# Source rows of two edge networks: windows of 28 and 56 columns in place of seven of 28, one core of a Trainium2

## The chip, the core and the metric

The kernel runs on one core of a Trainium2 chip. Its time is the device time of one execution in microseconds (us). Three runs took 1854.54, 1861.17 and 1861.94 us; the median is 1861.17 us.

## What is computed

Four small graph networks run one after the other on 100,000 nodes of 32 features and 25,000 directed edges, sorted by destination. After each, the node rows are added or replaced and normalised:

```python
x = _layernorm(x + _L0_gnn_ref(x, edge_weight, edge_attr_3, edge_index, ...))
x = _layernorm(x + _L1_gnn_ref(x, edge_index))
x = _layernorm(x + _L2_gnn_ref(x, edge_index, edge_attr_32, ...))
x = _layernorm(x + _L3_gnn_ref(x, edge_attr3_2x32, src, dst, ...))
```

The change touches the third and the fourth, the two edge networks (layers 0 and 1 of `compact` and `WINDOW_ORDER` in the code). Both need the row of each edge's source node, `x[src]`, in its newest state. In the third an MLP of source row, destination row and edge attributes is followed by a maximum over the edges of a destination (`segment_max`). The fourth is an attention: scores, a softmax over the edges of a destination, messages, and a sum over them.

## The kernel before

**Layout.** Edge e lies in partition e // 196, column e % 196: 128 partitions by T = 196 columns, of 32 words each. `A_src` holds the source rows, `A_dst` the destination rows. A chunk is 28 columns (`GATHER_CHUNK`), seven of them; a quad is four columns, 49 of them.

**Source rows.** A node that is nobody's destination keeps a row that each core step can derive from the old one; only sources that are themselves destinations have to be read again, from a table in DRAM (`tables[3]`, `tables[4]`). By a count of the drawn inputs that is 22% of the edges. GpSimd (POOL) reads them with indirect DMAs (`gather`, L746), one for each column of 128 rows. So that it needs fewer than 196, the indices are packed: `make_windows` sorts them within each window of 28 columns to the window's first 16 places (`SLOTS_IN_WINDOW`), and DVE later moves the rows back to their own columns. Ahead of each gather stands a memset of a small tile that POOL itself waits for (`pause`, L736). If any window of any partition had more than 16 such sources, `n_short` would be set to T and the code would take its long branches.

**Moving.** `move_window(layer, c, k)` issues step k of window c: predicated copies (`copy_predicated`, L2253) that shift rows to the right by 16, 8, 4, 2 and 1 columns, of 12, 20, 24, 26 and 27 columns of 32 words, by masks from `make_windows`, and a last one (L2249) that puts the rows of all 28 columns in place. Step 0 first waits on DVE for the gathers of that window (`window_rows`). DVE's instructions run in the order of the code, so all that is written behind this wait waits with it.

**Order of work.** DVE, PE and ACT go through the network in turns, a quad each (`pipeline`); behind a turn, steps are hooked in by its number. In the third network turns 0 and 1 are the last two quads (columns 188 to 195) and turn q + 2 is quad q, up to turn 51 with the pipeline's lag. `bring_rows` (L2264) copies the quad's rows for PE, `take_maxima` (L2276, a scan over a chunk) follows behind turns 4, 11, 18, 25, 32, 39 and 46, the norm of each chunk after it (`center`, `variance`, `scale`). The windows are gathered in the order 6, 0, 1, ..., 5 (`WINDOW_ORDER`); windows 6 and 0 are moved in one go, window c = 1 to 5 in the six turns from 7c - 4 on. In the fourth network turn q is quad q (`bring_both`, L2368, and `score`); `HOOKS` gives the turns of the hooked steps: window c = 1 to 6 is moved behind turns 7c - 6 to 7c - 1, the softmax of chunk c behind turn 7c + 12, its messages are normalised behind 7c + 15 (L1495 with 56 words out), and the chunk's last step, `scale`, at 7c + 25 releases `final_ready`.

**End.** POOL scatters the finished rows of the fourth network to the output, one indirect DMA a column (L880), in the order of `LAST_ORDER`: columns 8 to 27, then chunks 1 to 6, then columns 0 to 7; ahead of each it waits for `final_ready`. These 196 scatters stand in POOL's queue behind the gathers of the fourth network.

## Time and profile before

| | |
|---|---|
| median of three runs | 1861.17 us |
| profiled execution, its span | 1863.2 us |
| POOL busy | 1400.9 us, 75% |
| DVE busy | 1344.3 us, 72% |
| PE busy | 729.3 us, 39% |
| ACT busy | 488.0 us, 26% |
| third network | 1084.6 us to 1359.2 us |
| fourth network | 1359.2 us to the end |

The times of the rows below come from one profiled execution; its span, from the first to the last instruction, is 1863.2 us and is its only time. POOL and DVE are both busy for about three quarters of it, and neither all the time: which of them sets the pace has to be read stretch by stretch. A third network's start is taken where DVE begins to spread the rows over the edges of a destination, and its end where it begins to do so for the fourth.

### The profile page before, as it was taken

Reading aid. Unit: us, or ns where it says so; the run is one execution under the profiler, and the core shown is the slowest. Engines: PE = TensorE matmul, PEld = TensorE weight load, DVE = VectorE, ACT = ScalarE, POOL = GpSimd, SP = SyncE. Lnnn points to the kernel's source line nnn. Section 1 sums busy time; section 2 is a strip of 40 time slices with the busy share of each in tenths; the row PEclk is TensorE's granted clock in tenths of the full one; section 3 lists DMA queues with packets and bytes.
Section 4 is the critical chain, followed back from the end, with each engine's and each line's share of the span. In section 5 each row is a group of like instructions: output and inputs, shape, how many; then the busy total and the mean of one; then the engine's idle time right before and its main releaser. Section 6 shows DMA issues by size and latency. Waiting matters only on the chain.

```text
span 1863.2 us, 14783 instructions
## 1 busy us (share of the span) xinstructions
PE 729.3 (39%) x3676; PEld 546.2 (29%) x3676; DVE 1344.3 (72%) x2600; ACT 488.0 (26%) x1014; POOL 1400.9 (75%) x2019
## 2 busy tenths in 40 slices
PE   7912555541450003605337001456605656551400
PEld 3301222220220003605326001355505655551400
DVE  9955999986999645775755882478785999986400
ACT  7822311110110013522334200233302343342100
POOL 8878887888888885868878558884068888888776
PEclk9966778775785556867678555677757776665655
DMA  8165511111111101412222330000001111110000
GB/s 321 38 211 194 184 32 32 32 26 17 26 20 50 42 20 59 137 65 76 99 88 102 140 137 4 5 23 13 30 20 24 32 28 26 32 29 9 10 10 10
DMA packets 64097, 114.29 MB, mean 61 GB/s; under 512 B 27599, under 2 KB 48648, under 8 KB 63224
## 3 DMA queue, kind: packets, MB, share of 16 engines
q1 hardware_dynamic: 24304, 80.96, 12.0%
q0 software_dynamic: 33728, 12.79, 4.9%
q10 hardware_dynamic: 5960, 19.43, 2.8%
q8 instruction: 31, 0.51, 0.1%
q14 instruction: 74, 0.61, 0.1%
HBM read 61.66 MB, written 55.21 MB: 63 GB/s over the span
## 4 chain that ended last, share of the span: by engine, by line
POOL 75%; issue 17%; DVE 5%; PE 1%; DMA 1%; ACT 0%; POOLq 0%; SPq 0%; DVEq 0%
POOL A_dst L746 12%; POOL A_src L746 12%; POOL out L880 12%; POOL gtmp L736 9%; POOL work L746 8%; POOL A_msg L746 7%; POOL A_msg L823 7%; POOL edge_sums L829 5%; POOL out_short L746 3%; DVE A_dst L1484 1%; DVE stat L1495 1%; DVE work L2276 0%; DVE A_sum L1484 0%; PE bank L1388 0%; DVE A_dst L1492 0%
## 5 line engine op out<-in xcount | busy, mean ns | idle before, releaser
L746 POOL DMA_INDIRECT A_dst<-in_x,dst_i x196 | 224.3, 1144 | 57.4 <-POOL gtmp L736 39.1
L736 POOL MEMSET gtmp<- 64x64 f32 x934 | 156.5, 168 | 144.6 <-DMA table<-A_dst 110.9
L880 POOL DMA_INDIRECT out<-A_dst,out_i x196 | 217.9, 1112 | 59.7 <-POOL gtmp L736 34.3
L1495 DVE TENSOR_REDUCE work<-work 128x80 f32<-128x1280 f32 (+3 forms) x147 | 204.6, 1421 | 78.8 <-issue 50.2
L1310 PE MATMUL bank<-w2fold,work 128*128 128x384 f32 x392 | 183.1, 611 | 173.0 <-DVE work L1484 162.7
L746 POOL DMA_INDIRECT A_src<-x_pos,A_tmp x140 | 147.2, 1051 | 40.5 <-POOL gtmp L736 24.4
L746 POOL DMA_INDIRECT work<-table,pos_i x112 | 144.9, 1294 | 31.1 <-POOL gtmp L736 23.5
L1235 PE MATMUL bank<-ident,work 128*128 128x128 f32 (+1 forms) x294 | 63.4, 327 | 264.1 <-ACTq L995 139.2
L1310 PEld LDWEIGHTS bank<-w2fold,work 128*128 128x128 f32 x392 | 86.0, 237 | 269.5 <-issue 227.1
L746 POOL DMA_INDIRECT A_msg<-table,pos_i x112 | 139.0, 1241 | 32.4 <-POOL gtmp L736 16.5
L1484 DVE TENSOR_TENSOR work<-bank,work 128x384 f32<-128x384 f32 (+1 forms) x294 | 153.6, 590 | 0.2
L975 ACT ACTIVATE work<-A_tmp,b1col,w1col 65x256 f32<-65x256 f32 x98 | 58.3, 599 | 322.5 <-PE bank L1310 275.6
L1348 PE MATMUL bank<-nodes_w,small 128*128 128x128 f32 (+1 forms) x784 | 116.8, 306 | 63.2 <-ACT small L1006 59.2
L1348 PEld LDWEIGHTS bank<-nodes_w,small 128*128 128x128 f32 (+1 forms) x784 | 106.6, 215 | 72.9 <-ACT small L1006 67.1
L1235 PEld LDWEIGHTS bank<-ident,work 128*128 128x128 f32 (+1 forms) x294 | 41.8, 172 | 268.4 <-issue 165.1
L1235 PE MATMUL bank<-ident,end_col 128*32 128x128 f32 (+2 forms) x18 | 6.8, 379 | 271.1 <-DVE end_col L1540 239.1
L1235 PE MATMUL bank<-ident,A_tmp 128*65 128x128 f32 (+1 forms) x203 | 43.6, 355 | 123.7 <-DVE A_tmp L2369 113.8
L823 POOL DMA_INDIRECT A_msg<-table,nxt_i x60 | 74.4, 1239 | 17.9 <-POOL gtmp L736 9.3
L746 POOL DMA_INDIRECT A_src<-in_x,A_tmp x56 | 73.3, 1309 | 16.9 <-issue 16.9
L829 POOL DMA_INDIRECT edge_sums<-A_sum,out_short x60 | 72.0, 1200 | 17.9 <-POOL gtmp L736 12.2
L1235 PEld LDWEIGHTS bank<-ident,end_col 128*32 128x32 f32 (+2 forms) x18 | 1.7, 95 | 274.8 <-DVE end_col L1540 241.7
L1261 PE MATMUL bank<-A_msg,A_sum 128*128 128x392 f16 x392 | 80.0, 338 | 1.6 <-ACT A_sum L929 1.6
(396 smaller groups left out, 2335.5 us busy)
## 6 DMA issues: line engine op xcount, KB each, us to landing
work<-in_x SPq DMA_DIRECT2D x26, 960.0 KB
x_pos<-A_sum SPq DMA_DIRECT2D x13, 990.0 KB
out<-work ACTq DMA_DIRECT2D x13, 960.0 KB
A_tmp<-ew_turned_rows ACTq DMA_DIRECT2D x49, 130.0 KB
table<-A_dst SPq DMA_DIRECT2D x2, 3136.0 KB
edge_sums<-A_dst SPq DMA_DIRECT2D x2, 3136.0 KB
table<-A_dst SPq DMA_DIRECT2D x13, 448.0 KB
A_tmp<-in_edge_attr_2x SPq DMA_DIRECT2D x49, 112.0 KB
```

The costliest lines, as they stand in the source:

```text
L736: pool.memset(tile, 0.0).then_inc(cleared, 1)
L746: pool.indirect_dma_start(out=column(t), out_offset=None, in_=of, in_offset=bass.IndirectOffsetOnAxis(ap=idx[:, t:t + 1], axis=0), bounds_ ...
L823: return lambda t: pool.indirect_dma_start(out=column(t), out_offset=None, in_=of, in_offset=bass.IndirectOffsetOnAxis(ap=idx[:, t:t + 1], ...
L829: return lambda t: pool.indirect_dma_start(out=of, out_offset=bass.IndirectOffsetOnAxis(ap=idx[:, t:t + 1], axis=0), in_=column(t), in_off ...
L880: pool.indirect_dma_start(out=out, out_offset=bass.IndirectOffsetOnAxis(ap=out_i[:, t:t + 1], axis=0), in_=A_dst[:, t, :], in_offset=None, ...
L975: nc.scalar.activation(hidT[:, u % PAIRS_DEEP, :], ew_all[:, q % EW_SLOTS, slot * 2 * P:(slot + 1) * 2 * P], ACT.Relu, bias=b1col[:], scal ...
L1235: return nc.tensor.transpose(out_ap, in_ap, ident[0:n, 0:n])
L1261: last = nc.tensor.matmul(banks[6 + h][:, 0:half], lo_hot[:, 2 * slot + j, :], hi_hot[:, 2 * slot + j, h * half:(h + 1) * half], start=Fal ...
L1310: last = nc.tensor.matmul(banks[2 * (u % PAIRS_DEEP) + j][:, 0:PATHS], hid_rows[:, u % PAIRS_DEEP, j * P:(j + 1) * P], w2_rows[:], start=T ...
L1348: last = nc.tensor.matmul(node_products(i, w)[0:parts, k * P:(k + 1) * P], n_xT[:, s, k * parts:(k + 1) * parts], nodes_w[:, w * P:(w + 1) ...
L1484: return v.tensor_tensor(out=o, in0=a, in1=b, op=op)
L1495: return v.tensor_reduce(out=o, in_=a, axis=AX, op=op)
```

## The change

In place of seven windows of 28 columns with 16 places each there are four: columns 0 to 27 with 16 places, and 28 to 83, 84 to 139 and 140 to 195 with 28 places each (`WINDOWS`). A window of 56 columns is moved in seven steps, shifts of 32, 16, 8, 4, 2 and 1 of 24, 40, 48, 52, 54 and 55 columns, and the last of 56. `STEPS` is 7, and the windows' steps stand behind the seven turns ahead of the window's first quad. `make_windows` packs by six bits in place of five and makes masks for both kinds of window; `make_short` compares each window's count with its own places.

```diff
 FIRST_OUT = [12, 24, 36]
 TOP = -(-T // 8) * 8
 SLOTS = 2
-SLOTS_IN_WINDOW = 16
-MOVES = [(16, 12), (8, 20), (4, 24), (2, 26), (1, 27)]
+WINDOWS = [(0, 28, 16), (28, 56, 28), (84, 56, 28), (140, 56, 28)]
+WINDOW_KINDS = [(0, 1, 28, 16), (28, 3, 56, 28)]
+SHIFT_BITS = 6
+
+
+def moves_of(width, slots):
+    moves, reach = [], slots
+    for shift in (32, 16, 8, 4, 2, 1):
+        if shift < width:
+            moves.append((shift, min(reach, width - shift)))
+            reach = min(reach + shift, width)
+    return moves
...
-        WINDOW_ORDER = [[CHUNKS - 1, *range(CHUNKS - 1)], [*range(CHUNKS)]]
+        WINDOW_ORDER = [[len(WINDOWS) - 1, *range(len(WINDOWS) - 1)], [*range(len(WINDOWS))]]
+
+        def window_count(layer, i):
+
+            return 16 * sum(WINDOWS[w][2] for w in WINDOW_ORDER[layer][i % SLOTS:i + 1:SLOTS])
+
+        STEPS = len(moves_of(*WINDOWS[1][1:])) + 1

...
-        HOOKS = dict({f"move_{k}": k - len(MOVES) - 1 for k in range(len(MOVES) + 1)}, soft_max=12, exp_scores=13, weights=13, exp_rows=14, normalise=15, turn=16, take_turned=17, product=18,
+        HOOKS = dict({f"move_{k}": k - STEPS for k in range(STEPS)}, soft_max=12, exp_scores=13, weights=13, exp_rows=14, normalise=15, turn=16, take_turned=17, product=18,
                      take_product=19, sums=20, add=21, square=22, variance=23, root=24, scale=25)
...
                 pool.sem_inc(wide_in, 1)
-                for i, c in enumerate(order):
+                for i, w in enumerate(order):
+                    first, _, slots = WINDOWS[w]
                     here = window_rows[k - 3][i % SLOTS]
                     if i >= SLOTS:
-                        pool.wait_ge(here, 16 * SLOTS_IN_WINDOW * (i // SLOTS))
+                        pool.wait_ge(here, window_count(k - 3, i - SLOTS))
                     gather(lambda t: of[:, t, :], tables[k], pos_i, edge_limit, lambda t: here,
-                           range(c * GATHER_CHUNK, c * GATHER_CHUNK + SLOTS_IN_WINDOW), cleared_tile=gtmp[0:HF])
+                           range(first, first + slots), cleared_tile=gtmp[0:HF])

...
+                for bit in range(SHIFT_BITS):
+                    shift = 1 << bit
                     step(v.tensor_copy(win_bits, win_row))
                     step(ts(win_bits, win_bits, shift, ALU.bitwise_and))
                     step(stt(win_moved, win_bits, 0.0, win_row, ALU.is_gt, ALU.mult))
                     step(tt(win_row, win_row, win_moved, ALU.subtract))
-                    if shift == 1:
-                        step(ts(move_masks[0], rows, 0.0, ALU.is_gt))
-                    step(ts(move_masks[shift], moved[:, :, shift:shift + n], 0.0, ALU.is_gt))
-                    left_of = slice(0, GATHER_CHUNK - shift)
-                    step(tt(rows[:, :, left_of], rows[:, :, left_of], moved[:, :, shift:], ALU.add))
+                    for kind, masks in enumerate(move_masks):
+                        if shift not in masks:
+                            continue
+                        rows, moved = by_window(win_row, kind), by_window(win_moved, kind)
+                        if shift == 1:
+                            step(ts(masks[0], rows, 0.0, ALU.is_gt))
+                        step(ts(masks[shift], moved[:, :, shift:shift + masks[shift].shape[2]], 0.0, ALU.is_gt))
+                        left_of = slice(0, rows.shape[2] - shift)
+                        step(tt(rows[:, :, left_of], rows[:, :, left_of], moved[:, :, shift:], ALU.add))
                 step(v.tensor_copy(win_bits, win_row))
-                step(ts(win_bits, win_bits, 5, ALU.arith_shift_right))
+                step(ts(win_bits, win_bits, SHIFT_BITS, ALU.arith_shift_right))
                 step(ts(win_rank, win_bits, 0.0, ALU.is_equal, float(SKIP), ALU.mult))
                 step(ts(win_column, win_bits, -1.0, ALU.add))
                 step(tt(pos_i[:], win_column, win_rank, ALU.add))
...
-            def move_window(layer, c, k):
-
-
-                rows, base = compact[layer], c * GATHER_CHUNK
+            def move_window(layer, w, k):
+
+
+                base, width, slots = WINDOWS[w]
+                kind = [k for k, at in enumerate(WINDOW_KINDS) if at[0] <= base][-1]
+                rows, masks, here = compact[layer], move_masks[kind], (base - WINDOW_KINDS[kind][0]) // width
+                moves = moves_of(width, slots)
+                k -= STEPS - 1 - len(moves)
+                if k < 0:
+                    return
                 if k == 0:
-                    i = WINDOW_ORDER[layer].index(c)
                     v.wait_ge(wide_in, layer + 1)
-                    v.wait_ge(window_rows[layer][i % SLOTS], 16 * SLOTS_IN_WINDOW * (i // SLOTS + 1))
-                if k == len(MOVES):
-                    all_of = slice(base, base + GATHER_CHUNK)
-                    step(v.copy_predicated(A_src[:, all_of, :], bcast(move_masks[0][:, c, :], FEAT), rows[:, all_of, :]))
+                    i = WINDOW_ORDER[layer].index(w)
+                    v.wait_ge(window_rows[layer][i % SLOTS], window_count(layer, i))
+                if k == len(moves):
+                    all_of = slice(base, base + width)
+                    step(v.copy_predicated(A_src[:, all_of, :], bcast(masks[0][:, here, :], FEAT), rows[:, all_of, :]))
                     return
-                shift, n = MOVES[k]
+                shift, n = moves[k]
                 to = A_src if shift == 1 else rows
                 step(v.copy_predicated(to[:, base + shift:base + shift + n, :][:, ::-1, :],
-                                       bcast(move_masks[shift][:, c, ::-1], FEAT), rows[:, base:base + n, :][:, ::-1, :]))
-
-            def bring_window(layer, c):
-
-                for k in range(len(MOVES) + 1):
-                    move_window(layer, c, k)
+                                       bcast(masks[shift][:, here, ::-1], FEAT), rows[:, base:base + n, :][:, ::-1, :]))
+
+            def bring_window(layer, w):
+
+                for k in range(STEPS):
+                    move_window(layer, w, k)
...
                 after.setdefault(QUADS - 1, []).append(partial(scale_sources, CHUNKS - 1))
-                for c in range(1, CHUNKS - 1):
-                    for k in range(len(MOVES) + 1):
-                        after.setdefault(7 * c - 4 + k, []).insert(0, partial(move_window, 0, c, k))
+                for w in WINDOW_ORDER[0][2:]:
+                    for k in range(STEPS):
+                        first_turn = END_QUADS + WINDOWS[w][0] // 4
+                        after.setdefault(first_turn - STEPS + k, []).insert(0, partial(move_window, 0, w, k))
                 after.setdefault(1, []).append(partial(bring_window, 0, 0))
-                bring_window(0, CHUNKS - 1)
...
                 after, late = in_time([
-                    *((f"move_{k}", lambda c, k=k: move_window(1, c, k), range(1, CHUNKS)) for k in range(len(MOVES) + 1)),
+                    *((f"move_{k}", lambda c, k=k: move_window(1, [at[0] for at in WINDOWS].index(c * GATHER_CHUNK), k),
+                       [WINDOWS[w][0] // GATHER_CHUNK for w in WINDOW_ORDER[1][1:]]) for k in range(STEPS)),
                     ("soft_max", soft_max, early), ("weights", weights, early),
```

Two places in DVE's order show what moves. The first is the start of the third network. `work` is `compact[0]` here, `A_sum` the destination rows. Before, behind the windows that are moved in one go:

```order
L2264 COPY work<-A_sum 128x4x32
L1484 TENSOR_TENSOR work<-A_src,small 128x4x32
L2264 COPY work<-A_sum 128x4x32
L1484 TENSOR_TENSOR work<-A_src,small 128x4x32
L2253 COPY_PREDICATED work<-near_masks,work 128x12x32
L2264 COPY work<-A_sum 128x4x32
L1484 TENSOR_TENSOR work<-A_src,small 128x4x32
L2253 COPY_PREDICATED work<-nodes_t,work 128x20x32
L2276 SCALAR_TENSOR_TENSOR work<-work 128x928
```

The pairs of copy and multiplication are turns 2, 3 and 4, and window 1 begins behind turn 3. Of the change, the same place (lines have moved by 35 and 19):

```order
L2299 COPY work<-A_sum 128x4x32
L1503 TENSOR_TENSOR work<-A_src,small 128x4x32
L2288 COPY_PREDICATED work<-near_masks,work 128x24x32
L2299 COPY work<-A_sum 128x4x32
L1503 TENSOR_TENSOR work<-A_src,small 128x4x32
L2288 COPY_PREDICATED work<-near_masks,work 128x40x32
L2299 COPY work<-A_sum 128x4x32
L1503 TENSOR_TENSOR work<-A_src,small 128x4x32
L2288 COPY_PREDICATED work<-nodes_t,work 128x48x32
L2311 SCALAR_TENSOR_TENSOR work<-work 128x928
```

The first step of the window of columns 28 to 83, and with it the wait for its 28 gathers, stands behind turn 2. The next window, of columns 84 to 139, stands behind turn 16; window 5, the last one gathered before, stood behind turn 31.

The second place is the start of the fourth network, behind the window of columns 0 to 27. Before:

```order
L2368 COPY A_tmp<-A_src 128x4x32
L2369 COPY A_tmp<-A_sum 128x4x32
L2368 COPY A_tmp<-A_src 128x4x32
L2369 COPY A_tmp<-A_sum 128x4x32
L2253 COPY_PREDICATED A_msg<-near_masks,A_msg 128x12x32
```

And of the change:

```order
L2404 COPY A_tmp<-A_src 128x4x32
L2405 COPY A_tmp<-A_sum 128x4x32
L2288 COPY_PREDICATED A_msg<-near_masks,A_msg 128x24x32
L2404 COPY A_tmp<-A_src 128x4x32
L2405 COPY A_tmp<-A_sum 128x4x32
L2288 COPY_PREDICATED A_msg<-near_masks,A_msg 128x40x32
```

The wait for the second window has moved from behind turn 1 to behind turn 0; the third window (84 to 139) begins behind turn 14 and the fourth (140 to 195) behind turn 28.

## Rows read from the trace of the kernel before

**Rows 1.** The page's chain of work that ended last, by engine.

```profile
POOL 75%; issue 17%; DVE 5%; PE 1%; DMA 1%; ACT 0%; POOLq 0%; SPq 0%; DVEq 0%
```

**Rows 2.** POOL in order of time: start, duration in us, what, idle before.

```profile
1116.26 1.00 POOL L746 DMA_INDIRECT work<-table,pos_i  x1 [0.27 <-POOL gtmp L736]
...
1117.70 1.00 POOL L746 DMA_INDIRECT work<-table,pos_i  x1 [0.27 <-POOL gtmp L736]
...
1131.01 1.91 POOL L746 DMA_INDIRECT work<-table,pos_i  x1 [0.27 <-POOL gtmp L736]
```

**Rows 3.** DVE in order of time, third network, first copies of windows.

```profile
1127.14 0.58 DVE L2253 COPY_PREDICATED work<-near_masks,work 128x384 f32<-128x384 uint8 x1 [13.19 <-DMA work<-table,pos_i]
...
1151.45 0.59 DVE L2253 COPY_PREDICATED work<-near_masks,work 128x384 f32<-128x384 uint8 x1 [17.30 <-DMA work<-table,pos_i]
...
1283.97 0.59 DVE L2253 COPY_PREDICATED work<-near_masks,work 128x384 f32<-128x384 uint8 x1 [4.96 <-DMA work<-table,pos_i]
```

**Rows 4.** Stretches: length, then busy us of PE, PEld, DVE, ACT, POOL.

```profile
1175.70:1202.00 26.30, 14.78 (x84) 13.71 (x84) 12.33 (x24) 8.10 (x22) 21.95 (x33) 0.69 0.04 5
1202.00:1230.70 28.70, 15.95 (x86) 14.23 (x86) 22.43 (x40) 9.46 (x24) 24.08 (x35) 0.68 0.08 21
1256.80:1284.00 27.20, 15.69 (x84) 14.30 (x84) 20.36 (x33) 9.59 (x24) 21.89 (x31) 0.75 0.08 21
```

**Rows 5.** DVE in order of time: scans of three chunks, start of fourth network.

```profile
1285.84 2.09 DVE L2276 TENSOR_TENSOR_SCAN work<-work 128x928 f32<-128x928 f32 x1
...
1308.33 2.09 DVE L2276 TENSOR_TENSOR_SCAN work<-work 128x928 f32<-128x928 f32 x1 [1.81 <-ACT work L1099]
...
1329.22 2.09 DVE L2276 TENSOR_TENSOR_SCAN work<-work 128x928 f32<-128x928 f32 x1 [1.81 <-ACT work L1099]
...
1359.24 6.69 DVE L1484 TENSOR_TENSOR work<-A_dst,is_last 128x6272 f32<-128x6272 f32 x1
```

**Rows 6.** DVE in order of time, fourth network, first copies of windows.

```profile
1392.18 0.58 DVE L2253 COPY_PREDICATED A_msg<-near_masks,A_msg 128x384 f32<-128x384 uint8 x1 [4.42 <-DMA A_msg<-table,pos_i]
...
1416.41 0.58 DVE L2253 COPY_PREDICATED A_msg<-near_masks,A_msg 128x384 f32<-128x384 uint8 x1 [17.43 <-DMA A_msg<-table,pos_i]
...
1442.67 0.58 DVE L2253 COPY_PREDICATED A_msg<-near_masks,A_msg 128x384 f32<-128x384 uint8 x1 [1.74 <-DMA A_msg<-table,pos_i]
```

**Rows 7.** DVE in order of time: messages of chunks 3, 4 and 5 normalised.

```profile
1598.56 2.02 DVE L1495 TENSOR_REDUCE r<-work 128x56 f32<-128x1792 f32 x1
...
1640.89 2.01 DVE L1495 TENSOR_REDUCE r<-work 128x56 f32<-128x1792 f32 x1
...
1680.63 2.01 DVE L1495 TENSOR_REDUCE r<-work 128x56 f32<-128x1792 f32 x1
```

**Rows 8.** DVE in order of time: rows of chunks 0, 1, 2 made ready.

```profile
1532.28 0.82 DVE L1484 TENSOR_TENSOR A_dst<-A_dst,std 128x640 f32<-128x640 f32 x1
...
1574.73 1.09 DVE L1484 TENSOR_TENSOR A_dst<-A_dst,std 128x896 f32<-128x896 f32 x1
...
1617.68 1.09 DVE L1484 TENSOR_TENSOR A_dst<-A_dst,std 128x896 f32<-128x896 f32 x1
```

**Rows 9.** POOL in order of time: first scatters of chunks 0, 1, 2.

```profile
1552.33 1.37 POOL L880 DMA_INDIRECT out<-A_dst,out_i  x1 [0.28 <-issue]
...
1587.28 2.50 POOL L880 DMA_INDIRECT out<-A_dst,out_i  x1 [0.28 <-POOL gtmp L736]
...
1636.53 0.98 POOL L880 DMA_INDIRECT out<-A_dst,out_i  x1 [0.28 <-issue]
```

**Rows 10.** Groups of DVE copies: count, busy us, mean ns, idle before.

```profile
L2249 DVE COPY_PREDICATED A_src<-near_masks,work 128x896 f32<-128x896 uint8 x7 | 8.3, 1186 | 0.1
...
L2253 DVE COPY_PREDICATED work<-near_masks,work 128x384 f32<-128x384 uint8 x7 | 4.1, 586 | 73.3 <-DMA work<-table,pos_i 73.3
```

**Rows 11.** DVE in order of time: two waits in the first and second network.

```profile
657.09 1.09 DVE L1484 TENSOR_TENSOR A_dst<-A_dst,A_sum 128x896 f32<-128x896 f32 x1 [18.32 <-DMA A_dst<-in_x,dst_i]
...
1060.89 1.09 DVE L1492 SCALAR_TENSOR_TENSOR A_dst<-A_tmp,A_dst 128x896 f32<-128x896 f32 x1 [4.31 <-DMA A_tmp<-edge_sums]
```

More of the change, by code:

```diff
@@ L224, in gnn_kernel @@
         zero_hot = sb("zero_hot", [P, P], f16)
-        near_masks = sb("near_masks", [P, 4 * P], mybir.dt.uint8)
+        near_masks = sb("near_masks", [P, 6 * P], mybir.dt.uint8)
         far_masks = nodes_t[:].bitcast(mybir.dt.uint8)
@@ L347, in gnn_kernel, with by_window @@
         hi_digit, lo_digit, minus_lo = cv(P, T), cv(P, T), cv(P, T)
-        def by_window(ap):
-            return ap.rearrange("p (c t) -> p c t", t=GATHER_CHUNK)
-        move_masks, at = {}, {False: 0, True: 0}
-        for shift, n in [*MOVES, (0, GATHER_CHUNK)]:
-            far = shift in (8, 4, 2)
-            words = (far_masks if far else near_masks[:])[:, at[far]:at[far] + CHUNKS * n]
-            at[far] += CHUNKS * n
-            assert at[far] <= 4 * P
-            move_masks[shift] = words.rearrange("p (c t) -> p c t", t=n)
+        def by_window(ap, kind):
+            first, n, width, _ = WINDOW_KINDS[kind]
+            return ap[:, first:first + n * width].rearrange("p (c t) -> p c t", t=width)
+        move_masks, at = [{} for _ in WINDOW_KINDS], {False: 0, True: 0}
+        for kind, (_, windows, width, slots) in enumerate(WINDOW_KINDS):
+            for shift, n in [*moves_of(width, slots), (0, width)]:
+                far = width > GATHER_CHUNK and shift in (8, 4, 2)
+                words = (far_masks if far else near_masks[:])[:, at[far]:at[far] + windows * n]
+                at[far] += windows * n
+                assert at[far] <= (4 if far else 6) * P
+                move_masks[kind][shift] = words.rearrange("p (c t) -> p c t", t=n)
         in_window = source_var = small[:, 0, :]
@@ L1773, in make_short @@
                 step(v.memset(in_window, 1.0))
-                step(v.memset(by_window(in_window)[:, :, 0:1], 0.0))
+                for kind in range(len(WINDOW_KINDS)):
+                    ins = v.memset(by_window(in_window, kind)[:, :, 0:1], 0.0)
+                step(ins)
                 step(scan1(run, kept, in_window))
+                for kind, (_, _, _, slots) in enumerate(WINDOW_KINDS):
+                    ins = ts(by_window(run, kind), by_window(run, kind), float(-slots), ALU.add)
+                step(ins)
                 step(total(carry[:, 0:1], run, ALU.max))
-                step(ts(carry[:, 0:1], carry[:, 0:1], float(SLOTS_IN_WINDOW), ALU.is_gt, float(T), ALU.mult))
+                step(ts(carry[:, 0:1], carry[:, 0:1], 0.0, ALU.is_gt, float(T), ALU.mult))
                 v.memset(kept[:, 0:1], 1.0)
@@ L1940, in make_windows @@
                 step(tt(win_column, win_column, win_rank, ALU.subtract))
-                step(ts(win_rank, pos_i[:], 32.0, ALU.mult, 32.0, ALU.add))
+                step(ts(win_rank, pos_i[:], float(1 << SHIFT_BITS), ALU.mult, float(1 << SHIFT_BITS), ALU.add))
                 step(tt(win_rank, win_rank, win_column, ALU.add))
                 step(tt(win_row, win_rank, win_kept, ALU.mult))
-                rows, moved = by_window(win_row), by_window(win_moved)
-                for shift, n in reversed(MOVES):
+                for bit in range(SHIFT_BITS):
+                    shift = 1 << bit
                     step(v.tensor_copy(win_bits, win_row))
@@ L2207, in _ @@
             r1, alone = small[:, 1, :], small[:, 2, :]
-            by_column = by_window(alone)
-            step(ts(by_column, move_masks[0], -1.0, ALU.mult, 1.0, ALU.add))
-            step(stt(by_column[:, :, 1:], move_masks[1], -1.0, by_column[:, :, 1:], ALU.mult, ALU.add))
+            for kind, masks in enumerate(move_masks):
+                by_column = by_window(alone, kind)
+                step(ts(by_column, masks[0], -1.0, ALU.mult, 1.0, ALU.add))
+                step(stt(by_column[:, :, 1:], masks[1], -1.0, by_column[:, :, 1:], ALU.mult, ALU.add))
             v.wait_ge(std_ready, count["root"])
@@ L2307, in _ @@
             with v.If(ends_reg[0] > ENDS):
-                for c in WINDOW_ORDER[0]:
-                    bring_window(0, c)
+                for w in WINDOW_ORDER[0]:
+                    bring_window(0, w)
                 def pass_early():
@@ L2503, in _ @@
                 v.sem_inc(msg_ready, EARLY)
-                for c in range(CHUNKS):
-                    bring_window(1, c)
+                for w in WINDOW_ORDER[1]:
+                    bring_window(1, w)
                 pipeline(v, bring_both, None, score)
```

7 lines of the change are left out of this document (4 added, 3 removed).

## The prediction

> **What bounds the kernel now.** I read the profile page first, then the chain, then the time order of POOL and of DVE over the third and fourth network (from about 1084 us to the end). The chain is three quarters POOL, nearly all of it indirect DMAs [rows 1]: 128 rows gathered or scattered by each. So fewer gathers look like a straight gain. The time order of POOL gives the price of one: 1.00 us for the DMA instruction and 1.44 us from one gather to the next while DVE does little; beside a copy on DVE one took 1.91 us [rows 2].
>
> But the chain only names who came last. In the third network DVE waits for windows: 13.2 and 17.3 us at the first two, still 5.0 us at the last [rows 3]. Windows come 24.3 us apart early, and 27.1 us apart from 1256.85 to 1283.97 with DVE 20.4 us busy [rows 3, 4]; so a gather's 1.44 us grows by (27.1 - 23.0) / 20.4 = 0.2 us for each busy us of DVE. When the last window has landed at 1284.0, gathering is over and 75.3 us of DVE, PE and ACT work remain until the next network starts at 1359.2 [rows 3, 5]. What counts there is how many turns stand behind the last landing.
>
> In the fourth network DVE waits 4.4 and 17.4 us for its first two windows and 1.7 us for the third, and then never again for a window [rows 6]: from there DVE sets its own pace, 42.3 us for seven turns, and a stretch without copies still takes 39.7 us [rows 7]. POOL goes from the last gather straight to the scatters at 1552.3 [rows 8]. The scatters of a chunk need its rows ready: the first chunk's 20 columns are ready at 1532.28 + 0.82 = 1533.1, 19.2 us before POOL gets there; chunk 1 at 1575.8 against 1587.3, 11.5 us of slack; chunk 2 at 1618.8 against 1636.5, 17.7 us [rows 8, 9]. **If DVE falls behind POOL by more than 11.5 us, the end moves with DVE.**
>
> **What the change removes.** Per network 16 + 3 x 28 = 100 gathers where 7 x 16 = 112 stood: 12 fewer, 12 x 1.44 = 17.3 us of POOL, 34.6 us in both.
>
> **What it adds on DVE.** A copy takes 0.586 us for 384 words per partition and 1.186 us for 896 [rows 10]: 0.136 us + 1.17 ns per word. A short window (12, 20, 24, 26, 27 and 28 columns of 32 words) costs 0.59 + 0.89 + 1.04 + 1.11 + 1.15 + 1.19 = 6.0 us busy, 6.2 with gaps of some 0.03 us. A long one has copies of 24, 40, 48, 52, 54, 55 and 56 columns of 32 words: 1.04, 1.64, 1.94, 2.09, 2.16, 2.20, 2.24, together 13.3, with gaps 13.5 us. Per network 3 x 13.5 + 6.2 = 46.7 against 7 x 6.2 = 43.4 us: 3.3 us more. That is small. What matters is when copies and waits come.
>
> **What it moves, third network.** The order shows the long windows' first copies behind turns 2 and 16, and they are waits in DVE's own queue: behind the first wait stand all turns from 3 on, their PE and ACT work, and all maxima and norms. Landings, each worked out from the one before:
> - Columns 140 to 195, now first: 12 more gathers than at 1127.1 [rows 3]: 1144.4.
> - Columns 0 to 27: 24.3 us as before plus 1.3 for gathers held up by the longer copies: 1170.0. DVE has moved them by 1176 and then waits.
> - Columns 28 to 83: 24.3 + 17.3: 1211.6. DVE waited some 35 us at turn 2.
> - Columns 84 to 139: 28 x 1.44 = 40.3, plus 0.2 x 37 busy us = 7.4: **1259.3**. In the meantime DVE does what it did in two stretches before, 12.3 + 22.4 [rows 4], less 12.0 of short copies, plus 13.5: 36.2 us, some more with idle spots. It stands at turn 16 between 1248 and 1255 and waits, 4 to 11 us.
>
> So the last landing comes 24.7 us earlier than 1284.0, but with 15 more turns behind it (16 instead of 31). To the scan behind turn 18: three copies 4.6, two turns and the scaling of one chunk some 2.0, 1265.9. To the scan behind turn 25: 20.4 - 6.0 = 14.4 us of other work, 8.6 of copies, 1.6 idle, 1290.5. The next two stretches hold no copies; such a stretch took 20.9 us before, 1308.33 to 1329.22, since DVE then waits for ACT and PE [rows 5]: 1311.4 and 1332.3. Before, these two scans stood at 1285.8 and 1308.3. **The third network ends 24 us later, at 1383.** If the gathers were not slowed at all, the landing would be at 1252 and the end 7 us less late.
>
> **What it moves, fourth network.** Everything starts 24 us later; the first window is as before. The next one holds 28 gathers instead of 16, +17.3 us, and is waited for behind turn 0, not 1, with a copy longer by 0.45: at turn 2 DVE is 24 + 17.3 + 0.5 + 0.4 = 42.2 us late. It loses the wait of 1.7 us at the third window. Copies up to turn 32, where chunk 1 becomes ready: now 12.4 + 13.5 + 9.0 = 34.9 (the third long window's first five), before 5.6 + 3 x 6.2 + 3.6 = 27.8 (the fifth window's first four): +7.1. And a stretch freed of copies gives back only 42.3 - 39.7 = 2.6 of its 6.2 us [rows 7]: two stretches (turns 7 to 13 and 21 to 27) are freed; no row shows the first with ACT lightly loaded, so the loss is between 0 and 2 x 3.6 = 7 us; I take 2.5, since long copies also cover waits that stand there now. Lateness: chunk 0 (turn 25) 42.2 + 4.3 - 1.7 + 1.5 = 46.3, chunk 1 42.2 + 7.1 - 1.7 + 2.5 = **50.1**, chunk 2 42.2 + 5.4 - 1.7 + 3.5 = 49.4.
>
> POOL ends its gathers at 1552.3 + 24 - 17.3 = 1559 and waits until 1579.4 for chunk 0; 20 scatters take 35.0 as before [rows 9], 1614.4; it waits until 1625.9 for chunk 1; 28 scatters take 49.2, 1675, and chunk 2 is ready at 1668. From there POOL is the bound again. The end moves by 1625.9 - 1587.3 = 38.6, with about 1 more because DVE's work overlaps the scatters some 10 us longer.
>
> **What costs nothing.** The masks are built with 17 more small DVE instructions, ahead of a wait of 18 us for the first network's target rows; two more ahead of the third network's norm fall before a wait of 4.3 us for a DMA [rows 11]. Uncovered they would cost some 0.3 us each, 6 us. The wider test of the counts stays on the short path: counted from the inputs, no partition has more than 13 used rows in its first 28 columns (16 places), nor more than 19, 18 and 26 in the three longer windows (28 places).
>
> **Sum.** +39.5 us. The profiled execution's span, 1863.2 us, is 0.1% above the median of 1861.2; the shift is carried over whole: 1901 us, profiled span about 1903, 2.1% slower. A measurement of this kernel can tell about 0.5%, 9 us, from no change.
>
> **Rivals.**
> - *Copies hold up the gathers more.* Beside copies of 1.2 us a gather took 0.9 us longer [rows 2]. Copies of 2.2 us could each hold one up by 1.1 us more: five in each long window, 3 us beyond what I allowed, three times on the path: +9, 1910 us.
> - The Trainium skill, "SBUF — State Buffer", section "SBUF: two separate sides", says that VectorE and GpSimd share a port pair that one holds for its whole instruction, also a VectorE instruction with two SBUF inputs, while the other is fully blocked. By that rule each long copy can hold a gather to its end, and this rival holds; the gather of 1.91 us [rows 2] agrees with it, and no row here shows a copy of 2.2 us beside a gather.
> - *The third network drains at DVE's speed.* If a stretch without copies took 14.4 us instead of 20.9, 13 us less: 1888. Against it stand the idle spots in the one such stretch that the trace has.
> - *The windows are POOL's gain (other side).* If DVE's lateness stays under the 11.5 us of slack, for instance since its work drains behind each window as fast as rows land, POOL's 34.6 us come off: 1827. The lateness decides, and the wait for the fourth network's first long window alone, 17.3 us, is over it; only the third network could win it back, where work behind the last landing grows instead.
> - *Even.* The third network comes out as before (the 24.7 us of earlier landing cover 15 turns): lateness 26, less 11.5, +15: 1876. With the fourth's freed stretches giving all back, about no change.
>
> **Chances.** Forecast 0.68, more contention 0.10, quick drain 0.11, third network even 0.04, no change 0.03, gain 0.04. The first case alone runs from 1884 (no slowing of the gathers, -7; nothing lost in freed stretches, -2.5; third network less idle, -7) to 1909 (+4.5 for the freed stretches, +3 for gathers). With the two next to it the range is 1882 to 1914, which leaves out about 0.15. Slower by over 0.5%: 0.93; within: 0.03; faster: 0.04.
>
> **What would show it.** In the profile after: 100 gathers a network; a wait of DVE for a landing of about 35 us near 1177 and one of 4 to 11 us near 1252; landings near 1144, 1170, 1212, 1259; the third network's last norm at 1383; in the fourth a wait of some 34 us at the second window; POOL idle twice, about 20 us ahead of the first scatter and 11 us ahead of the 21st, and not later. A span over 1915 would mean contention; a third network that ends before 1370 would break the count of turns; a 21st scatter that waits for nothing would break the last step.

## The result, and the profile after

The changed kernel takes 1904.06 us (median of four runs, 1898.52 to 1908.02) beside 1859.10 us for the kernel before (median of four; the first three alone gave 1861.17 us): a ratio of 1.0241, with a 95% interval from 1.0219 to 1.0263. The profiled execution's span grew from 1863.2 to 1906.1 us. The forecast was 1901 us, with a profiled span of about 1903.

The page after: the span, the busy time of each engine, and the chain of work that ended last, by engine (for before: [rows 1]).

```profile
span 1906.1 us, 14692 instructions
...
PE 732.2 (38%) x3676; PEld 552.7 (29%) x3676; DVE 1355.7 (71%) x2592; ACT 487.3 (26%) x1014; POOL 1370.6 (72%) x1971
...
POOL 66%; issue 16%; DVE 13%; PE 3%; DMA 1%; ACT 1%; POOLq 0%; DVEq 0%
```

POOL is busy 30 us less and DVE 11 us more, and DVE's share of the last chain went from 5% to 13%. The page says who is in the chain now, not why; that stands in the order of time. DVE in the third network after: the first copies of the four windows with the wait ahead of each, four scans, and the start of the fourth network (for before: [rows 3, 5]).

```profile
1142.22 2.62 DVE L2288 COPY_PREDICATED work<-near_masks,work 128x768 f32<-128x768 uint8 x2 [30.43 <-DMA work<-table,pos_i]
...
1169.03 1.55 DVE L2288 COPY_PREDICATED work<-near_masks,work 128x384 f32<-128x384 uint8 x2 [12.78 <-DMA work<-table,pos_i]
...
1210.58 1.01 DVE L2288 COPY_PREDICATED work<-near_masks,work 128x768 f32<-128x768 uint8 x1 [34.88 <-DMA work<-table,pos_i]
...
1261.67 1.01 DVE L2288 COPY_PREDICATED work<-near_masks,work 128x768 f32<-128x768 uint8 x1 [6.52 <-DMA work<-table,pos_i]
...
1268.05 2.09 DVE L2311 TENSOR_TENSOR_SCAN work<-work 128x928 f32<-128x928 f32 x1
...
1294.72 2.09 DVE L2311 TENSOR_TENSOR_SCAN work<-work 128x928 f32<-128x928 f32 x1 [3.32 <-ACT work L1118]
...
1316.05 2.09 DVE L2311 TENSOR_TENSOR_SCAN work<-work 128x928 f32<-128x928 f32 x1 [1.81 <-ACT work L1118]
...
1336.97 2.09 DVE L2311 TENSOR_TENSOR_SCAN work<-work 128x928 f32<-128x928 f32 x1 [1.81 <-ACT work L1118]
...
1387.62 6.69 DVE L1503 TENSOR_TENSOR work<-A_dst,is_last 128x6272 f32<-128x6272 f32 x1
```

The last landing is 22 us earlier than at 1283.97 [rows 3], and the fourth network starts 28.4 us later than at 1359.24 [rows 5]. DVE waits 84.6 us for landings in this network. DVE in the fourth network after: the two windows it waits for, and the rows of chunks 0, 1 and 2 made ready (for before: [rows 6, 8]).

```profile
1420.50 1.50 DVE L2288 COPY_PREDICATED A_msg<-near_masks,A_msg 128x384 f32<-128x384 uint8 x2 [4.25 <-DMA A_msg<-table,pos_i]
...
1462.00 1.01 DVE L2288 COPY_PREDICATED A_msg<-near_masks,A_msg 128x768 f32<-128x768 uint8 x1 [34.95 <-DMA A_msg<-table,pos_i]
...
1586.57 0.82 DVE L1503 TENSOR_TENSOR A_dst<-A_dst,std 128x640 f32<-128x640 f32 x1
...
1630.46 1.09 DVE L1503 TENSOR_TENSOR A_dst<-A_dst,std 128x896 f32<-128x896 f32 x1
...
1672.47 1.09 DVE L1503 TENSOR_TENSOR A_dst<-A_dst,std 128x896 f32<-128x896 f32 x1
```

POOL after, in order of time: its last gather, and the pause and first scatter of chunks 0 and 1, and the first scatter of chunk 2 (for before: [rows 9]).

```profile
1565.89 1.01 POOL L764 DMA_INDIRECT A_msg<-table,pos_i  x1 [0.27 <-POOL gtmp L754]
...
1587.45 0.16 POOL L754 MEMSET gtmp<- 64x64 f32 x1 [20.55 <-DVE A_dst L1503]
1587.89 1.03 POOL L899 DMA_INDIRECT out<-A_dst,out_i  x1 [0.28 <-POOL gtmp L754]
...
1631.62 0.16 POOL L754 MEMSET gtmp<- 64x64 f32 x1 [8.05 <-DVE A_dst L1503]
1632.05 0.98 POOL L899 DMA_INDIRECT out<-A_dst,out_i  x1 [0.28 <-POOL gtmp L754]
...
1679.18 1.00 POOL L899 DMA_INDIRECT out<-A_dst,out_i  x1 [0.28 <-POOL gtmp L754]
```

POOL stands idle twice, 20.6 and 8.1 us, and never again for DVE's rows: chunk 2 is ready at 1673.6, 5.6 us before its turn. From chunk 1 on the scatters run much as before, only later: from the first of chunk 1 to the first of chunk 2 it is 47.1 us, where it was 49.2.

### The profile page after: what moved, and what is told of

It reads as the page before. It is cut to its first block, busy times and chain, and to the rows that moved or that the text cites. A ratio compares the mean times of both kernels' runs of the same rounds, so it can differ in the third digit from the quotient of the medians.

```text
span 1906.1 us, 14692 instructions
## 1 busy us (share of the span) xinstructions
PE 732.2 (38%) x3676; PEld 552.7 (29%) x3676; DVE 1355.7 (71%) x2592; ACT 487.3 (26%) x1014; POOL 1370.6 (72%) x1971
## 4 chain that ended last, share of the span: by engine, by line
POOL 66%; issue 16%; DVE 13%; PE 3%; DMA 1%; ACT 1%; POOLq 0%; DVEq 0%
POOL A_dst L764 12%; POOL A_src L764 11%; POOL out L899 10%; POOL gtmp L754 8%; POOL work L764 7%; POOL A_msg L841 7%; POOL edge_sums L847 5%; POOL out_short L764 3%; POOL A_msg L764 3%; DVE A_dst L1503 2%; DVE work L1503 1%; DVE A_msg L2288 1%; DVE A_tmp L1503 1%; DVE stat L1514 1%; DVE r L1514 1%
## 5 line engine op out<-in xcount | busy, mean ns | idle before, releaser
L764 POOL DMA_INDIRECT A_msg<-table,pos_i x100 | 131.3, 1313 | 29.0 <-POOL gtmp L754 27.6
L764 POOL DMA_INDIRECT work<-table,pos_i x100 | 130.0, 1300 | 27.9 <-POOL gtmp L754 27.9
```

The lines of the kernel that those rows point to most:

```text
L764: pool.indirect_dma_start(out=column(t), out_offset=None, in_=of, in_offset=bass.IndirectOffsetOnAxis(ap=idx[:, t:t + 1], axis=0), bounds_ ...
```

## The experiments

Theory: DVE's lateness at chunk 1, past a slack of 11.5 us, sets the end; it comes from the long first waits and from the longer copies, while the gathers themselves give POOL's time back. Rivals: the longer copies slow POOL's gathers and that is the loss; or the last scatters depend on something else and the lateness is only a companion.

**Fewer gathers, nothing else.** Kernel before with 14 places in six windows and 16 in the last: 100 gathers a network as in the change, seven windows of 28 columns as before.

```diff
-SLOTS_IN_WINDOW = 16
+SLOTS_OF = [14] * 6 + [16]
...
-                           range(c * GATHER_CHUNK, c * GATHER_CHUNK + SLOTS_IN_WINDOW), cleared_tile=gtmp[0:HF])
+                           range(c * GATHER_CHUNK, c * GATHER_CHUNK + SLOTS_OF[c]), cleared_tile=gtmp[0:HF])
```

> The kernel before with 14 places instead of 16 in windows 0 to 5 (16 stay in window 6, which the drawn inputs fill): 100 gathers a network as in the change, but seven short windows, short copies and the old places of the waits. Theory (the end moves with DVE's lateness at the landings, and fewer gathers help where no landing is made coarser): every landing of the third network comes 2 x 1.44 us earlier per window, its end 17 us earlier; in the fourth another 3 us at each of the first two windows; POOL reaches the scatters 35 us earlier, and chunk 1 is ready just in time. 33 us faster than before, about 1826 us. Rival (fewer gathers are worth nothing, since DVE is the bound in both networks): within 5 us of before.

Measured: 1827.43 us, ratio 0.983 [0.9798, 0.9863]. The third network takes 254.6 us, 20 less than before (17 expected), and chunk 1 is ready at 1551.8 in place of 1575.8. The rival that fewer gathers are worth nothing falls: where nothing else changes they are a gain of 32 us, and the change gives away about 77 us against this kernel.

**The coarse order in one network or in both.** The kernel just shown, with the waits of 56-column windows but the short copies: in the third network windows 5 and 6 are gathered first and waited for together, and windows 1 and 3 wait for 2 and 4 too, one turn earlier. In the fourth windows 1, 3 and 5 do the same with 2, 4 and 6. The edit, shortened, against the kernel before:

```diff
-        WINDOW_ORDER = [[CHUNKS - 1, *range(CHUNKS - 1)], [*range(CHUNKS)]]
+        WINDOW_ORDER = [[5, 6, 0, 1, 2, 3, 4], [*range(CHUNKS)]]
...
                     v.wait_ge(wide_in, layer + 1)
-                    v.wait_ge(window_rows[layer][i % SLOTS], 16 * SLOTS_IN_WINDOW * (i // SLOTS + 1))
+                    for w in (c, *with_it):
+                        i = WINDOW_ORDER[layer].index(w)
+                        v.wait_ge(window_rows[layer][i % SLOTS], window_count(layer, i))
```

> As the first, with the landings of the third network made as coarse as in the change: windows 5 and 6 are gathered first and waited for together, then 0, then 1 and 2 are waited for together behind turn 2, 3 and 4 together behind turn 16; each is still moved by its own short copies. Theory: the last landing (the same 100 gathers) comes at about 1262 with turns 17 to 51 behind it, the third network ends 24 us later than before, 41 us later than in the first run; the fourth network gives back 6 us at its first two windows and its 11.5 us of slack; about 6 us slower than before, 1866 us, 40 slower than the first run. Rival (the long copies are what costs): as the first run, 1826.

> As the first, with only the fourth network's landings made coarse: windows 1 and 2 waited for together behind turn 0, 3 and 4 behind turn 14, 5 and 6 behind turn 28; short copies. Theory: the third network ends 17 us earlier, the first long wait of the fourth costs 17.8 us, chunk 1 is ready 4 us earlier than before, POOL waits for it and the end is 15.5 us earlier than before: 1844 us, 18 us slower than the first run. Rival (slack hides this wait, the cost of the change lies in the third network): as the first run, 1826.

> Both networks coarse, short copies: the change with nothing but its long copies and its two kinds of masks taken out. Theory: third network +24 us, fourth +17.8 - 2.9 - 1.7 us, less 11.5 us of slack: 26 us slower than before, 1885 us; the change (45 us slower) then owes 19 us to its long copies, 6 of them in the third network and 9 or 10 up to turn 32 of the fourth, and 3 to a first window of 16 gathers instead of 14. Rival (copies cost only their 3.3 us a network): within 8 us of the change, 1896 or more. Rival (copies are most of it): no more than 10 us slower than before.

| kernel | time, us | ratio [interval] | third network | its end to chunk 1 ready | chunk 1 ready |
|---|---|---|---|---|---|
| before | 1859.10 | 1 | 274.6 | 216.6 | 1575.8 |
| fewer gathers | 1827.43 | 0.983 [0.9798, 0.9863] | 254.6 | 210.2 | 1551.8 |
| + third coarse | 1872.83 | 1.0111 [1.0057, 1.0164] | 294.7 | 211.7 | 1588.6 |
| + fourth coarse | 1850.42 | 0.9951 [0.9935, 0.9966] | 256.9 | 234.6 | 1576.3 |
| + both | 1885.89 | 1.0153 [1.0124, 1.0182] | 292.1 | 232.5 | 1608.8 |
| the change | 1904.06 | 1.0241 [1.0219, 1.0263] | 305.1 | 243.9 | 1631.5 |

(The three right columns are of each kernel's profiled execution.) The waits alone, with the old copies, cost 58 us: 37 to 40 in the third network's length and 21 to 24 in the fourth's. The rest of the change adds 18: its long copies, and a first window of 16 gathers in place of 14, some 3 us of them by the price of a gather. That with both coarse was forecast at 1885 us and took 1885.89, so the rival that the longer copies cost only their 3.3 us a network falls too, and so does the one that they are most of it. Taken singly the two networks fit less well. The fourth alone costs 23 us against fewer gathers where 18 were expected. The third alone costs 45 us by the medians and 38 in the profiled executions where 40 were expected; its four runs lie between 1867.32 and 1888.41 us. Where these few us go is open. In the profiled executions the two parts, 38 and 23 us, add up to about what both cost together, 56, since no kernel of the table but the first has slack left at chunk 1: POOL waits for it in all of them, 3.0 us already with fewer gathers alone. POOL with both coarse, the pause ahead of chunk 1:

```profile
1608.86 0.16 POOL L739 MEMSET gtmp<- 64x64 f32 x1 [7.69 <-DVE A_dst L1487]
```

**A delay of DVE alone.** Kernel before with memsets of a spare tile on DVE behind turn 2 of the fourth network, each waiting for the one before: 10 of them, or 25.

```diff
+                after.setdefault(2, []).extend([lambda: step(v.memset(run_words, 0.0))] * 10)
                 pipeline(v, bring_both, None, score, after=after)
```

> The kernel before with ten memsets of 0.98 us each on DVE behind turn 2 of the fourth network, work that nobody needs. Theory: 9.8 us of lateness, less the wait of 1.7 us at the third window, is 8 us, under the slack of 11.5 us: the time stays within 2 us of before, 1860 us. Rival (DVE is the bound of the fourth network): 8 us or more slower, 1868.

> The same with 25 memsets, 24.5 us. Theory: 24.5 - 1.7 - 11.5 = 11.3 us slower than before, 1871 us, with POOL waiting ahead of the first and the 21st scatter. Rival (DVE is the bound): 23 us slower, 1882. Rival (POOL is the bound, DVE's work lies beside it): no slower.

Measured: 10 memsets 1867.93 us, ratio 1.0007 [0.9994, 1.0021]; 25 memsets 1886.10 us, ratio 1.0111 [1.0066, 1.0156]. In the trace one took 1.09 us, start to start, and the next turn began 14.4 us and 30.8 us after the one before, where it was 3.5 us: 10.9 and 27.3 us later. The first is under the slack of 11.5 us and costs nothing; the second is 15.8 us over it and costs 21 us (12 to 29). The forecast of 11 us was too low, since it took a memset at 0.98 us and took off a wait of 1.7 us. The interval of the second is wide enough for DVE as the bound as well, so the profiled execution has to decide: its span is 22.3 us longer, of which 6.1 us stand ahead of the fourth network (it starts at 1365.4 in place of 1359.2), and 16.2 us are left for a delay of 27.3. So lateness at chunk 1 is by itself enough to move the end; memsets read no row and gather nothing. POOL's pause ahead of chunk 1 with ten memsets:

```profile
1586.16 0.16 POOL L736 MEMSET gtmp<- 64x64 f32 x1 [7.55 <-DVE A_dst L1484]
1586.60 0.98 POOL L880 DMA_INDIRECT out<-A_dst,out_i  x1 [0.28 <-POOL gtmp L736]
```

The scatter comes at 1586.60, no later than before, but POOL has waited 7.6 us for it. It got there sooner, with its first scatter at 1547.40 in place of 1552.33: the time at which POOL arrives varies too, and in this execution the slack was used up.

**The changed kernel without copies.** `move_window` returns behind its waits. This leaves out putting the re-read source rows in place; edges whose source is a destination use its old row. It was run twice, on two chips.

```diff
                     v.wait_ge(window_rows[layer][i % SLOTS], window_count(layer, i))
+                return
```

> The change with all predicated copies of the windows left out, the waits for the landings kept: moved source rows are not put in place. Theory (waits for coarse landings are most of the cost): the third network still takes 12 us longer than before, 287 us, though 43 us of DVE work are gone; POOL's gathers of it take 165 us instead of 174, as no copy holds them up; the fourth gains 2.6 us for each seven turns; about as slow as before, 1860 us. Rival (the longer copies are the cost): as fast as the first run or faster, 1827 or less.

> The same kernel as the one with no copies, once more on another chip. There the third network took its expected 284 us, but in the fourth the hand-overs between TensorE and ScalarE took 2 to 3 us each from 1463 us to 1527 us, and a turn 7 to 10 us where 3.6 stand before; that was some 35 us. First theory: those stretched hand-overs belong to this execution or this chip and not to the missing copies; without them the third network ends at 1373 us and the window that holds chunk 1 is ready some 218 us after it (216.6 in the kernel before), at 1591 us, so the span is about 1867 us. Second theory: they come with the missing copies, and the run stays at 1900 to 1910 us.

Measured: 1907.50 us the first time, ratio 1.0196 [1.0139, 1.0253], and 1855.34 us the second, ratio 0.9977 [0.9961, 0.9992], with a span of 1858.5 us where about 1867 was expected. The first missed its forecast by 47.5 us, and the trace shows where. The third network took 283.9 us (expected 287). In the fourth, from 1463 to 1527 us, most hand-overs between TensorE and ScalarE took 2 to 4 us in place of 0.2 to 0.7 us. ScalarE in that stretch of the first run, then the same three lines of code in the second (in brackets the idle time ahead of each):

```profile
1472.34 0.38 ACT L1151 ACTIVATE A_tmp<-bank 128x256 f32<-128x256 f32 x1 [2.31 <-PE bank L1440]
1475.24 0.27 ACT L1155 COPY A_dst<-bank 128x128 f32<-128x128 f32 x1 [2.51 <-remote]
1477.48 0.58 ACT L1146 COPY A_tmp<-bank 65x512 f32<-65x512 f32 x1 [1.98 <-issue]
```

```profile
1457.47 0.38 ACT L1151 ACTIVATE A_tmp<-bank 128x256 f32<-128x256 f32 x1 [0.31 <-PE bank L1440]
1458.28 0.27 ACT L1155 COPY A_dst<-bank 128x128 f32<-128x128 f32 x1 [0.43 <-PE bank L1445]
1458.77 0.58 ACT L1146 COPY A_tmp<-bank 65x512 f32<-65x512 f32 x1 [0.22 <-PE bank L1254]
```

Nine turns of DVE took 70.8 us in the first (1464.0 to 1534.8) and the same nine 30.1 us in the second (1455.4 to 1485.5), 40.7 us of the 52.3 us between the two spans; another 7.2 us stand ahead of the fourth network, and the kernel before was itself 7.7 us slower on the first chip (1867.91 against 1860.17 us). So the miss belongs to that chip or those executions, and not to the missing copies; what stretches the hand-overs stays open. Undisturbed, the copies of both networks are worth 1904.1 - 1855.3 = 48.7 us. This kernel also speaks against another cause, a lower TensorE clock: the mean granted clock was 0.673 in the profiled execution of the change beside 0.685 before, but 0.672 in this one.

**Copies left out in the fourth network only** (there edges whose source is a destination use its old row).

```diff
+                if layer == 1:
+                    return
                 if k == len(moves):
```

> The changed kernel with the copies of the source rows left out in the fourth network only (edges whose source is a destination use the old rows there). The third network is that of the changed kernel and ends at 1387 to 1388 us. My theory, that the copies up to turn 32 delay the fourth network by their own time: three windows' copies, 13.5 + 6.2 us and two thirds of 13.5, some 28 us, go, and the run takes about 1878 us. The rival, that the fourth network is held by its gathers and the later order alone and the copies lie in waits: no more than 10 us go, 1896 us. If the stretched hand-overs between TensorE and ScalarE come with missing copies, 1905 us or more.

Measured: 1875.11 us, ratio 1.0087 [1.0062, 1.0112]. By the medians the fourth network's copies are worth 29 us (28 expected), and the rival that they lie in waits falls. From its start to chunk 1 ready this network takes 220.6 us in place of 243.9, so the trace gives them 23.3 us; most of the rest is the third network, which the edit leaves alone and which took 299.4 us here and 305.1 in the change. The 20 us left between this kernel and the one with no copies at all are the third network's copies; by the traces, 299.4 against 284.7 us, they are 14.6.

**Thirteen places.** The first kernel of this section with `[13] * 6 + [16]`, 94 gathers a network; also run twice.

> The first run's kernel with 13 places in windows 0 to 5, which is what the drawn inputs fill at most: 94 gathers a network, POOL has another 2 x 8.6 = 17 us less to do. Theory: the third network is then nearly DVE's (its stretches hold 22 to 26 us of DVE work against 21 to 26 us of gathers), ends some 5 us earlier than in the first run; the fourth wins 3 us at its first two windows; chunk 1's readiness, not POOL, sets the end: 9 us faster than the first run, 1818 us. Rival (POOL is the bound in the first run): 17 us faster, 1810 us.

> The kernel of before with 13 places in six windows (94 gathers a network) once more on another chip. The first theory (the stretched hand-overs are a thing of the execution) says 1818 to 1822 us, ratio 0.978 to 0.981, in nearly all its runs; the second (they come with these gathers) says 1860 us in most of them.

Measured: the first time three of four runs took 1859.76 to 1862.12 us and one 1820.96 us; the profiled execution, one of the three, shows the stretched hand-overs. No ratio can be given from that. The second time 1815.17 us over five runs (1810.98 to 1815.89; 1818 to 1822 expected), ratio 0.9758 [0.9737, 0.9779]. This is the fastest of all: 45.0 us off the kernel before, some 89 off the change. It has no places to spare: the fullest window of those six has 13 used rows by a count of the inputs, and one row more would send the kernel down its long branches. Against the kernel with 100 gathers it is some 12 to 13 us better where 12 fewer gathers are 17.3: POOL now waits for both chunks, so the next gain is DVE's to give. Those two pauses:

```profile
1494.99 0.16 POOL L739 MEMSET gtmp<- 64x64 f32 x1 [7.02 <-DVE A_dst L1487]
...
1536.86 0.16 POOL L739 MEMSET gtmp<- 64x64 f32 x1 [6.74 <-DVE A_dst L1487]
```

## Why the prediction was right

- **Gathers.** 100 a network, and 12 fewer give 32 us when nothing else changes, against 34.6 summed. POOL waits 3.0 us for chunk 1 in that kernel, about what is missing. Right.
- **Landings of the third network.** Forecast 1144.4, 1170.0, 1211.6 and 1259.3; measured 1142.2, 1169.0, 1210.6 and 1261.7. This execution's third network began 2.2 us earlier (1082.5 in place of 1084.6), so counted from its start they are 0.0, 1.2, 1.1 and 4.5 us late. The waits at turns 2 and 16 are 34.9 and 6.5 us (forecast 35, and 4 to 11). The excess is in one term, the stall of the gathers: 51.1 us for 28 gathers beside 34.75 us of busy DVE, (51.1 - 40.3) / 34.75 = 0.31 us per busy us, where 0.2 was taken. The kernel without the fourth's copies, with the same third network, gives 0.34 (52.1 us). The same stretch took 47.3 and 49.2 us with short copies (0.21 and 0.26), and 45.2 us with none (0.22, beside 22.1 busy us), so the 0.2 was right for short copies and the excess is the long ones'.

The stretch between the last two landings after: its length, then busy us of PE, PEld, DVE, ACT and POOL.

```profile
1210.60:1261.70 51.10, 28.80 (x170) 25.97 (x170) 34.75 (x57) 17.60 (x46) 42.03 (x55) 0.80 0.06 14
```

- **The end of the third network.** Forecast 1383, 24 us late; measured 1387.6, 28.4 late. From the last landing it took 125.9 us, forecast 123.7; the stretch to the scan behind turn 25 took 26.7 us and not 24.6, with a wait of 3.3 us for ACT that the estimate of 1.6 idle us had too small. The same network in the kernel without the fourth's copies took 299.4 us, and 298.4 was forecast: some 6 of the 305.1 us here vary between executions. Right, a little short.
- **The fourth network.** The wait at the second window was 34.95 us (forecast some 34). Lateness beyond the start: chunk 0 +25.9 us (forecast 22.3), chunk 1 +27.3 (26.1), chunk 2 +26.4 (25.4). The copies up to turn 32, 34.9 us by the sum, are confirmed only loosely, by 23.3 us of trace and 29 us of time when they go. Loss in freed stretches, taken as 2.5 of at most 7 us, was not measured by itself, and why chunk 0 came 3.6 us later than summed up is open.
- **The end.** POOL ends its gathers at 1566.9 (forecast 1559), waits 20.6 us for chunk 0 (20.4), 8.1 for chunk 1 (11), and for no later one. (The prediction cites rows 8 for the first scatter; it stands in rows 9.) The 21st scatter is 44.8 us late (forecast 38.6), chunk 2's first 42.7 and the span 42.9 (39.5): the scatters of chunk 1 ran 2.1 us quicker than before, so the "about 1 more" for overlap had the wrong sign.
- **What costs nothing.** Kernels with and without the new masks were not compared by themselves. The third network starts 2.2 us earlier after, so no loss shows ahead of it; but this start varies, from 1084.6 to 1091.4 us in three profiled executions with the old masks, so a few us could hide there.
- **The rivals.** *Copies hold up the gathers more* had the right mechanism, and about half its +9 us came on the path: the last landing of the third network was 4.5 us late, the second window of the fourth 1 us. The third network's 100 gathers took 173.8 and 171.9 us from first to last beside the long copies, 166.6 and 168.8 with short copies in the same order, 162.0 and 162.9 with none. POOL beside a long window's copies, and below it DVE's copies of the same time:

```profile
1219.18 2.62 POOL L764 DMA_INDIRECT work<-table,pos_i  x1 [0.27 <-POOL gtmp L754]
...
1222.24 2.04 POOL L764 DMA_INDIRECT work<-table,pos_i  x1 [0.27 <-POOL gtmp L754]
...
1224.71 2.24 POOL L764 DMA_INDIRECT work<-table,pos_i  x1 [0.27 <-POOL gtmp L754]
```

```profile
1218.94 2.02 DVE L2288 COPY_PREDICATED work<-nodes_t,work 128x1664 f32<-128x1664 uint8 x1
...
1221.34 2.09 DVE L2288 COPY_PREDICATED work<-nodes_t,work 128x1728 f32<-128x1728 uint8 x1
...
1223.81 2.31 DVE L2288 COPY_PREDICATED A_src<-near_masks,work 128x1760 f32<-128x1760 uint8 x1
```

The copies end at 1220.96, 1223.43 and 1226.12; the gathers, 1.00 us when alone, end at 1221.80, 1224.28 and 1226.95, 0.83 to 0.85 us later each. So it is with all 27 gathers of the two networks after that began within a copy which the timeline shows by itself: each ends 0.81 to 0.85 us after that copy's end, and the longest took 2.97 us. A gather is held to the end of the copy it meets, so a copy twice as long can hold it twice as long. The Trainium skill, "SBUF — State Buffer", section "SBUF: two separate sides", has a VectorE instruction with two SBUF inputs and a GpSimd instruction that reads SBUF keep each other off the shared port, the later one fully blocked until the first is done; the trace agrees with that at every such gather. The 0.2 and 0.3 us per busy us are averages over gathers that meet a copy and gathers that meet none. *The third network drains at DVE's speed* fell: its copy-free stretch took 20.9 us (1316.05 to the next scan at 1336.97), as before. *The windows are POOL's gain* and *even* fell with the lateness: 55.7 us at chunk 1 (forecast 50.1) against 11.5 of slack.

All in all the sum came out 3.4 us short in the profiled span and 5.3 us in the ratio (0.0241 of 1859.1 is 44.8 us, forecast 39.5), and the term that was mis-sized is the stall of gathers beside DVE's copies, taken as 0.2 and measured as 0.3 us per busy us, with ACT's wait in the stretch behind it. That the sum came out so close is in part luck: the third network's length varies by some 6 us between executions, and the scatters' 2.1 us offset part of the shortfall.

## What to carry to other kernels

Making a transfer's batches larger to save a few of them pays the sum of the batch's rows as a wait ahead of the first consumer; count the turns that stand behind the last landing, not the instructions saved. Before trusting a gain on the engine that fills the chain, read the slack between each release and its use (here 11.5 us at one chunk), because an engine that looks idle a quarter of the time can be 11 us from being the bound. And long copies beside a series of gathers hold each gather that they meet to their end. If fewer gathers are wanted, shrink the batches (13 places for 16, 2.4% faster here), as far as the inputs allow, and leave their number alone.

## What was not expected of the hardware

- The same 100 gathers with the same pauses took 162.0 to 176.3 us by what DVE did beside them. What counts is which DVE instruction a gather meets: beside predicated copies it ends 0.81 to 0.85 us after the copy (27 gathers), while 12 gathers that began beside a reduction (TENSOR_REDUCE) in the fourth network took 1.00 us like those alone. The third gather of the third network began beside 32 scans in a row and took 12.90 us, ending at 1104.92, 0.87 us after the last of them; before it is the same, 12.90 us.

```profile
1092.02 12.90 POOL L764 DMA_INDIRECT work<-table,pos_i  x1 [0.27 <-POOL gtmp L754]
```

```profile
1089.22 14.83 DVE L1602 TENSOR_TENSOR_SCAN A_sum<-not_last,A_msg 128x196 f32<-128x196 f32 x32
```

- Two kernels on one chip showed a stretch, of 64 us in one and some 45 us in the other, in which most hand-overs between TensorE and ScalarE took 2 to 4 us (0.2 to 0.7 us elsewhere). The granted TensorE clock in the first was 0.60 (1463 to 1527 us) beside 0.87 in the same turns of the undisturbed run (1455 to 1487 us), means over the levels 1.2 and 2.4 GHz. TensorE was busy 35.84 of its 64 us, in short pieces with waits between, so a lower clock may be the consequence; no run settles it. The same kernels on another chip did not show it. On the first chip 3 of 13 runs of the kernel before also took 1927 to 1930 us, some 60 us more than the rest, and one of ten with ten memsets 1933.72 us; no trace shows whether that is the same. A single time of such a run, read without its trace, would have turned the finding on the copies round.

First row: the stretch in the disturbed run. Second: the undisturbed one (columns as above, then the granted clock).

```profile
1463.00:1527.00 64.00, 35.84 (x180) 32.48 (x180) 21.69 (x70) 10.15 (x25) 51.50 (x87) 0.60 0.09 21
```

```profile
1455.00:1487.00 32.00, 24.48 (x194) 23.57 (x195) 29.76 (x92) 14.94 (x33) 26.30 (x43) 0.87 0.17 43
```
